# Routed attention experts: query, key and value weights held still, tokens streamed, values on the two column halves of the array

## The reference

```python
rw = _gating(hidden_states, sim_matrix, gates)          # 16 expert weights for each token
q = jnp.einsum('bte,bted->btd', rw, jnp.einsum('btc,ecd->bted', hidden_states, q_proj))
k = jnp.einsum('bte,bted->btd', rw, jnp.einsum('btc,ecd->bted', hidden_states, k_proj))
v = jnp.einsum('bte,bted->btd', rw, jnp.einsum('btc,ecd->bted', hidden_states, v_proj))
scores = jnp.einsum('bqd,bkd->bqk', q, k) * scale        # causal mask, softmax
attn = jnp.einsum('bqk,bkd->bqd', jax.nn.softmax(scores, axis=-1), v)
mixed = attn[:, :, None, :] * rw[..., None]
return jnp.einsum('bted,edc->btc', mixed, o_proj)
```

## Time and profile before

| | |
|---|---|
| runs | 1598.56, 1603.86, 1604.44 us, median 1603.86 us |
| the profiled execution's own time | 1601.31 us |
| its span, first to last instruction | 1599.5 us |
| mean granted TensorE clock | 0.935 |
| PE busy | 1390.7 us (87%) |
| PEld busy | 1019.3 us (64%) |
| DVE busy | 1144.8 us (72%) |
| ACT, POOL busy | 529.0 us, 531.6 us |
| first routed layer | about 383 to 725 us |
| second routed layer | about 1238 us to the end |

### The profile page before, as it was taken

The page is one execution under the profiler, slowest core; times in us unless marked ns, Lnnn a source line. Parts: engine busy times, 40 slices in busy tenths (PEclk is TensorE's granted clock), DMA queues, the critical chain, the costliest instruction groups (busy, mean ns, idle before and its releaser), DMA issues.

```text
span 1599.5 us, 21272 instructions
## 1 busy us (share of the span) xinstructions
PE 1390.7 (87%) x7178; PEld 1019.3 (64%) x7178; DVE 1144.8 (72%) x2582; ACT 529.0 (33%) x1015; POOL 531.6 (33%) x446
## 2 busy tenths in 40 slices
PE   2896886599999999986988988898987689999997
PEld 2793454588899999972333333343332689999996
DVE  3786674477677777532799999999998657777753
ACT  2203443210222222214556556556542022222221
POOL 1150000000000000001798999998996000000000
PEclk9998999699999999987899999999988799999999
DMA  4560000455333333300333332332331333333330
GB/s 146 208 211 0 1 1 1 145 192 194 107 107 107 107 107 107 107 1 22 101 94 87 99 99 89 99 105 86 96 105 40 107 107 113 113 113 114 114 114 14
DMA packets 93162, 155.11 MB, mean 97 GB/s; under 512 B 11703, under 2 KB 21374, under 8 KB 92926
## 3 DMA queue, kind: packets, MB, share of 16 engines
q1 hardware_dynamic: 93054, 153.76, 30.0%
HBM read 150.31 MB, written 3.41 MB: 96 GB/s over the span
## 4 chain that ended last, share of the span: by engine, by line
PE 63%; DVE 15%; issue 10%; POOL 6%; ACT 3%; DMA 2%; SPq 0%; DVEq 0%; POOLq 0%; ACTq 0%
PE bank L1103 21%; PE bank L1106 7%; PE bank L1218 6%; PE bank L960 4%; POOL both L603 3%; PE bank L991 3%; PE bank L1063 2%; DVE hs L1574 2%; PE bank L1048 2%; PE bank L1115 2%; PE bank L1157 2%; PE bank L1045 2%; DVE xe L1574 2%; DVE xe L1397 2%; PE bank L1000 2%
## 5 line engine op out<-in xcount | busy, mean ns | idle before, releaser
L1103 PE MATMUL bank<-wqkv_sb,xe 128*128 128x192 f32 x2048 | 368.4, 332 | 8.2 <-DVE xe L1517 8.2
L1103 PEld LDWEIGHTS bank<-wqkv_sb,xe 128*128 128x128 f32 x2048 | 337.5, 193 | 20.0 <-DVE xe L1517 11.3
L1218 PE MATMUL bank<-both,ident 128*128 128x512 f32 x512 | 262.3, 640 | 44.6 <-DVE both L1566 44.6
L571 POOL TENSOR_TENSOR rstd<-ve,half_neg 128x4 f32<-128x4 f32 x32 | 37.9, 1184 | 728.1 <-DVE ve L1272 728.1
L861 ACT ACTIVATE bank<-dt,A 128x512 f32<-128x512 f32 x256 | 176.1, 688 | 167.5 <-DVE hs L1574 88.9
L1218 PEld LDWEIGHTS bank<-both,ident 128*128 128x128 f32 x512 | 101.8, 206 | 172.1 <-issue 104.0
L603 POOL TENSOR_TENSOR both<-du,prT 128x512 f32<-128x512 f32 x128 | 160.9, 1272 | 7.3 <-DMA prT<-bc_dram 6.8
L1574 DVE TENSOR_TENSOR_SCAN xe<-bank,both 128x512 f32<-128x512 f32 x128 | 153.7, 1209 | 11.4 <-ACT bank L861 11.4
L603 POOL TENSOR_TENSOR both<-du,prob 128x512 f32<-128x512 f32 x128 | 160.3, 1273 | 1.9 <-DVE hs L1574 1.2
L960 PE MATMUL bank<-exp_sb,xe 128*128 128x128 f32 x1024 | 130.7, 284 | 28.8 <-DVE xe L1397 28.2
L1574 DVE TENSOR_TENSOR_SCAN hs<-bank,both 128x512 f32<-128x512 f32 x128 | 153.1, 1207 | 1.2 <-ACT bank L861 1.2
(11 more groups left out here) (256 smaller groups left out, 1978.6 us busy)
## 6 DMA issues: line engine op xcount, KB each, us to landing
dt<-w_rows SPq DMA_DIRECT2D x128, 256.0 KB, 4.1
du<-w_rows SPq DMA_DIRECT2D x128, 256.0 KB, 4.7
prob<-bc_dram SPq DMA_DIRECT2D x64, 256.0 KB, 3.3
prT<-bc_dram SPq DMA_DIRECT2D x64, 256.0 KB, 3.3
dt<-g_dram SPq DMA_DIRECT2D x32, 256.0 KB, 6.1
du<-g_dram SPq DMA_DIRECT2D x32, 256.0 KB, 6.4
g<-g_dram SPq DMA_DIRECT2D x32, 256.0 KB, 6.8
u<-g_dram SPq DMA_DIRECT2D x32, 256.0 KB, 6.7
```

The lines of the kernel that those rows point to most:

```text
L571: pool.tensor_tensor(rstd[:], ve[:], half_neg[:, 0:NT], ALU.pow).then_inc(ln_rstd, 1)
L1103: m = pe.matmul(bank[4 + j // 2][:, (j % 2) * 3 * HD:(j % 2 + 1) * 3 * HD], x_e, wqkv_sb[:, e, :], start=(e == 0 and j % 2 == 0), stop=(e ...
L1218: pe.matmul(bank[4 + k % NH][:], ident[:], hc[k % HRING], start=False, stop=(SUM_RANK[k] == sums_of(k // UNITS, k % NH))).then_inc(hc_used, 1)
```

## The change

It does four things. The experts' q and k weights (128 columns together) become the stationary operand, and the whole weighted tile of 512 tokens is streamed past them into bank 4, which now holds q and k transposed. The v weights (64 columns) of four experts are used together after every fourth expert, alternately on array columns 0 to 63 and 64 to 127, into the two halves of bank 5. ScalarE copies q and k straight into `qT`, `kT`; v goes to `vT`, is turned on TensorE by a product with `ident2`, two 64 x 64 unit matrices above and beside each other (this also adds the two halves and doubles the result), and goes from bank 0 to `v2` in one copy. The ring of weighted tiles has eight slots in place of four, and in units 0 to 15 a slot is given back with its group of four.

```diff
+                for a in range(2):
+                    chain.link(pool.tensor_tensor(ident2[:, a, :], ident[:, 0:HD], ident[:, HD:P], ALU.add))
...
                 def back(b):
-                    act.wait_ge(qkT_ps, seen(n + 1))
-                    act.activation(qT[:], bank[0][0:HD, :], ACT.Copy).then_inc(qkT_sb, 1)
-                    act.activation(kT[:], bank[0][HD:P, :], ACT.Copy).then_inc(qkT_sb, 1)
-                    yield
...
                 def qkv_copies(b):
                     act.wait_ge(xe_used, seen(experts_at(r, b) + E2))
-                    for h in range(2):
-                        qkv = bank[4 + h][:, 0:2 * 3 * HD].rearrange("p (j c) -> p j c", j=2)
-                        act.activation(qk_sb[:, 2 * h:2 * h + 2, :], qkv[:, :, 0:P], ACT.Copy).then_inc(qkv_sb, 1)
-                        for d in range(2):
-                            act.activation(v2[:, 2 * h:2 * h + 2, d, :], qkv[:, :, P:3 * HD], ACT.Copy).then_inc(qkv_sb, 1)
+                    act.wait_ge(sc_ps, seen(NT * n))
+                    act.activation(qT[:], bank[4][0:HD, :], ACT.Copy).then_inc(qkT_sb, 1)
+                    act.activation(kT[:], bank[4][HD:P, :], ACT.Copy).then_inc(qkT_sb, 1)
+                    act.activation(vT[:], bank[5][:], ACT.Copy).then_inc(vT_sb, 1)
+
+                def v_copy(b):
+                    act.wait_ge(v_turn, seen(n + 1))
+                    act.wait_ge(at_ps, seen(NT * n))
+                    act.activation(v2[:].rearrange("p j a c -> p (j a c)"), bank[0][:], ACT.Copy).then_inc(v2_sb, 1)
...
+                    if u % UNIT == E2 + 4 and 0 <= u < UNIT * NB:
+                        v_copy(u // UNIT)
...
-                    pe.wait_ge(qkv_sb, seen(6 * (n + 1)))
+                    pe.wait_ge(qkT_sb, seen(2 * (n + 1)))
+                    scores(0)
+                    yield
+                    pe.wait_ge(vT_sb, seen(n + 1))
                     pe.wait_ge(pT_sb, seen(NT * n))
                     for j in range(NT):
-                        m = pe.transpose(bank[0][:, j * P:(j + 1) * P], qk_sb[:, j, :], ident[:])
-                    m.then_inc(qkT_ps, 1)
-                    yield
-                    pe.wait_ge(qkT_sb, seen(2 * (n + 1)))
-                    scores(0)
+                        m = pe.matmul(bank[0][:, j * P:(j + 1) * P], vT[:, j * P:(j + 1) * P], ident2[:].rearrange("p a c -> p (a c)"), start=True, stop=True)
+                    m.then_inc(v_turn, 1)
                     yield
...
-                    for j in range(NT):
-                        x_e = xe[i % RING][:, j * P:(j + 1) * P]
-                        if e < E2:
-                            m = pe.matmul(bank[4 + j // 2][:, (j % 2) * 3 * HD:(j % 2 + 1) * 3 * HD], x_e, wqkv_sb[:, e, :],
-                                          start=(e == 0 and j % 2 == 0), stop=(e == E2 - 1 and j % 2 == 1))
+                    if e < E2:
+                        pe.matmul(bank[4][:], wqkv_sb[:, e, 0:P], hs[i % HRING][:], start=(e == 0), stop=(e == E2 - 1))
+                        if e % 4 == 3:
+                            for d in range(4):
+                                m = pe.matmul(bank[5][HD * (d % 2):HD * (d % 2 + 1), :], wqkv_sb[:, e - 3 + d, P:3 * HD], hs[(i - 3 + d) % HRING][:],
+                                              start=(e == 3 and d < 2), stop=(e == E2 - 1 and d >= 2))
+                            m.then_inc(xe_used, 4)
...
-                        dve.wait_ge(xe_used, seen(base + i + 1 - RING))
+                        dve.wait_ge(xe_used, seen(base + i + 1 - HRING))
```

More of the change, by code:

```diff
@@ L298, in macaron @@
         rden = sb("rden", [P, NT])
-        qk_sb = sb("qk_sb", [P, NT, P])
+        vT = sb("vT", [P, L])
+        ident2 = sb("ident2", [P, 2, HD])
         v2 = sb("v2", [P, NT, 2, HD])
@@ L336, in macaron @@
         bcT3 = wT3
[L337 removed]
+        Cs = [at2[:], vT[:]]
         xn_odd = prob[0][:].rearrange("p (j c) -> p j c", j=NT)
@@ L389, in macaron @@
             sem(n) for n in ("qk_ps", "turn_used", "frac_made", "feat_made", "v_ps", "v_made", "s_ps", "p_made"))
-        qkv_sb, qkT_ps, qkT_sb, sc_ps, nmax_made, prob_made, pT_ps, pT_sb, at_ps, at_sb = (
-            sem(n) for n in ("qkv_sb", "qkT_ps", "qkT_sb", "sc_ps", "nmax_made", "prob_made", "pT_ps", "pT_sb", "at_ps", "at_sb"))
+        vT_sb, v_turn, v2_sb, qkT_sb, sc_ps, nmax_made, prob_made, pT_ps, pT_sb, at_ps, at_sb = (
+            sem(n) for n in ("vT_sb", "v_turn", "v2_sb", "qkT_sb", "sc_ps", "nmax_made", "prob_made", "pT_ps", "pT_sb", "at_ps", "at_sb"))
         nmr_made, bank7_ps, part_ps, dlt_sb, g_made, th_made, thr_made, u_made, Du_done, ez_made, ln_made, dt_made, gates_made, \
@@ L786, in qkv_copies @@
                 def qkv_copies(b):
+                    n = r * NB + b
                     act.wait_ge(xe_used, seen(experts_at(r, b) + E2))
-                    for h in range(2):
-                        qkv = bank[4 + h][:, 0:2 * 3 * HD].rearrange("p (j c) -> p j c", j=2)
-                        act.activation(qk_sb[:, 2 * h:2 * h + 2, :], qkv[:, :, 0:P], ACT.Copy).then_inc(qkv_sb, 1)
-                        for d in range(2):
-                            act.activation(v2[:, 2 * h:2 * h + 2, d, :], qkv[:, :, P:3 * HD], ACT.Copy).then_inc(qkv_sb, 1)
-                steps = by_clock(front, 1 if layer == 3 else 0, (6, 14, 17, 19), back, (18, 22, 23, 25, 26, 28, 29, 31, 32, 34))
+                    act.wait_ge(sc_ps, seen(NT * n))
[3 more added lines that the diff above has]
+                def v_copy(b):
+                    n = r * NB + b
+                    act.wait_ge(v_turn, seen(n + 1))
+                    act.wait_ge(at_ps, seen(NT * n))
+                    act.activation(v2[:].rearrange("p j a c -> p (j a c)"), bank[0][:], ACT.Copy).then_inc(v2_sb, 1)
+                steps = by_clock(front, 1 if layer == 3 else 0, (6, 14, 17, 19), back, (22, 23, 25, 26, 28, 29, 31, 32, 34))
                 for u in CLOCK:
@@ L1052, in turned @@
                         pe.wait_ge(prob_made, seen(NT * n + t + 1))
+                        if t == 0:
+                            pe.wait_ge(v2_sb, seen(n + 1))
                         pe.wait_ge(pT_sb, seen(NT * n + t))
@@ L1098, in unit @@
                     if e == 0:
-                        pe.wait_ge(qkv_sb, seen(6 * (r * NB + b)))
-                    for j in range(NT):
-                        x_e = xe[i % RING][:, j * P:(j + 1) * P]
-                        if e < E2:
-                            m = pe.matmul(bank[4 + j // 2][:, (j % 2) * 3 * HD:(j % 2 + 1) * 3 * HD], x_e, wqkv_sb[:, e, :],
-                                          start=(e == 0 and j % 2 == 0), stop=(e == E2 - 1 and j % 2 == 1))
-                        else:
-                            m = pe.matmul(bank[7][:, j * P:(j + 1) * P], x_e, wo2_sb[:, e - E2, :],
+                        pe.wait_ge(qkT_sb, seen(2 * (r * NB + b)))
+                        pe.wait_ge(vT_sb, seen(r * NB + b))
+                    if e < E2:
[5 more added lines that the diff above has]
+                            m.then_inc(xe_used, 4)
+                    else:
+                        for j in range(NT):
+                            m = pe.matmul(bank[7][:, j * P:(j + 1) * P], hs[i % HRING][:, j * P:(j + 1) * P], wo2_sb[:, e - E2, :],
                                           start=(e == E2 and j == 0), stop=(e == UNIT - 1 and j == NT - 1))
-                    m.then_inc(xe_used, 1)
+                        m.then_inc(xe_used, 1)
                 def spread(c, k):
@@ L1516, in routed @@
                             w = bank[2 + (e - E2) % 2][:]
-                        dve.tensor_tensor(xe[i % RING][:], xnT[b % 2][:] if e < E2 else at2[:], w, ALU.mult).then_inc(xe_made, 1)
+                        dve.tensor_tensor(hs[i % HRING][:], xnT[b % 2][:] if e < E2 else at2[:], w, ALU.mult).then_inc(xe_made, 1)
                     due(steps, u)
```

## The result

The changed kernel takes 1632.05 us (median of 4 runs, 1631.55 to 1633.16), the kernel before 1601.23 us (4 runs, 1598.56 to 1604.44) on the same chip. The ratio is 1.0199, with a 95% interval of 1.018 to 1.0218: 31 us or 2.0% slower, where +49 us (1651) was forecast, in a range from 1604 to 1728 and an own range of the likeliest case from 1628 to 1668.

What follows compares the result with a forecast made beforehand. The prediction took TensorE's own instruction sequence as the bound. Its terms, 34.9 (q, k and v products) + 7.2 (turning v) - 0.6 (ScalarE) + 7.5 (VectorE wait), gave +49.0 us, 1651 us, in a range from 1604 to 1728.

Steps and rivals of the forecast that it cites:

- the likeliest case: Staggered pairing of the v products' column halves, chance 0.45: +49.0 us, 1651 us, own range 1628 to 1668.
- the five steps with their loads: In a v group, eight instructions take five steps, 2.15 us, plus 0.165 us of weight loads.
- The bound and the sign: TensorE's own sequence sets the pace in the routed layers; equal columns streamed leave nothing large to win; slower 0.80.
- The v groups: Four experts' v products: 2.15 us plus 0.165 of loads; with q and k, +0.545 us a group, +34.9 us.
- they start in program order in every row: In v groups, each product's second instruction waits for its first and holds up later ones, giving five steps.
- they pair fully: Rival for v groups: hardware sorts each half's instructions, four steps, 1.72 us; 1612 us in total; chance 0.15.
- The mode's price: Going from full array to column halves and back: taken as 0, bound 0.2 us at each change, 25.6 us.
- The turning of v: On TensorE, four fp32 products replace four transposes: +0.45 us a batch in 16 batches, +7.2 us.
- The wait for VectorE: TensorE waits 0.5 us for the tile before a batch's third expert, 15 batches: +7.5 us, bounds 0 and 12.
- ScalarE and the first batches: ScalarE's copies cost nothing except behind a layer's first batch, where scores come earlier: -0.6 us for both layers.
- The ring of eight: Eight weighted-tile slots bring nothing: the wait before the third expert is VectorE's, and elsewhere there is none to remove.
- the 1692: Top of the range for staggered pairing in the v groups with the full price of mode changes.

Runs made afterwards that it cites:

- e2: Changed kernel with all four v products of a group on one column half (old values read in the other): 1743.96 us, ratio 1.090 to the kernel before.
- e4: Changed kernel with a group's v products on halves 0, 0, 1, 1 instead of alternating, ring slots reordered: 1633.56 us, ratio 1.021 to the kernel before.
- e3: Changed kernel with k and v together as a full-width stationary in the v products (computed v wrong): 1723.75 us, ratio 1.0774 to the kernel before.
- e1: Changed kernel with v products of two experts after every second expert, not four after every fourth: 1646.33 us, ratio 1.0291 to the kernel before.
- e7: Changed kernel with v turned by four transposes instead of four fp32 products (halves not added, attention wrong): 1626.24 us, ratio 1.0174 to the kernel before.
- e6: Changed kernel with VectorE's small routing steps ahead of the scores' maximum, ring slots renamed: 1626.28 us, ratio 1.0176 to the kernel before.
- e5: Kernel before with only the ring of eight weighted tiles added: 1597.55 us against 1596.35, ratio 1.000.
- e9: Kernel before with qT and kT zero-filled to 128 rows, so the scores use the whole array: 1565.22 us, ratio 0.9779.
- e10: Kernel before with scores on zero-filled 128 rows and VectorE's small routing steps ahead of the scores' maximum: 1566.26 us, ratio 0.9788.

## Why the prediction was right, step by step

**In short.** The direction and the bound were right, the mechanism of the v groups was not, and that 1632 us lies in the own range is partly luck: the five steps with their loads were 0.60 us a group too dear (38 us in 64 groups), the missing price of the mode 0.35 too cheap (22 us), and 3.7 us came off in the scan, whose work is the same as before.

**The bound and the sign: right.** TensorE sets the pace of these stages before and after; a batch rose by 2.20 us and the two layers by 35.5. The reason given for the sign holds in part: the same number of columns is streamed, and the loads that go away were hidden (37.28 to 24.29 us of load time for nothing), so nothing was to be won. Without the price of the mode, which the forecast left out, the v groups would have cost nothing either (64 x (3.43 + 1.72 - 5.20) = -3 us), and the slowdown would have been the turning of v and the waits alone.

**The v groups: right in place, wrong in mechanism, and 0.25 us a group too dear.** Said: five steps and 0.165 us of loads, 2.31 us, no price for the mode; sum 64 x 0.545 = +34.9. Found: four steps (e2 against changed: 1.71 us saved in a group; e4: per half in order, not over both) and 0.35 us for the mode (e2 against e3; e1), 2.07 us; 64 x (3.43 + 2.07 - 5.20) = +19.2, and +17 with the mean price of 0.32. The step that failed is "they start in program order in every row". In no row of before were two matmuls on different columns, so those rows could not tell. The rival "they pair fully" had the true number of steps; it lacked the mode's price, which the prediction kept as a bound of 0.4 us a group.

**The mode's price: wrongly taken as 0.** It was read from the transposes with 16 columns, which pass without a gap. They are fp32 transposes, and the Trainium skill, "TensorEngine Tiling (Array Packing)", Restrictions, names just these as what column tiling excludes ("Transpose mode (FP32/FP32R input)"). That would explain the missing gap; no run here tests it. The rule of that page's Key Properties that a change of mode drains the engine holds here for columns as for rows: 0.09 us of emptying at each change, and an unhidden fp32 load behind it, 0.05 for 64 columns, 0.10 for 128. The scores in the earlier trace rows were the row that answered, and the prediction had read it: 0.1 of emptying and 0.1 of load.

**The turning of v: right.** +0.45 us a batch said, 0.45 in e7.

**The wait for VectorE: right in place and size, in fewer batches.** 0.5 us before the third expert said; 0.55 measured (e6), in the ten batches of steady state and not in 15: +5.5 for +7.5.

**ScalarE and the first batches: wrong in sign.** Said -0.6 us. From a layer's first expert product to that of its second batch it took 33.5 us for 30.6 in the first routed layer and 34.9 for 32.4 in the second, +2.9 and +2.5. Four v groups and the turning account for 1.65 each; the rest is 2.1 us for both layers. In the first layer it goes with waits: TensorE's idle time in this stretch rose from 3.1 to 4.4 us, 1.09 of it before the second batch's first tile (at 418.85). In the second layer the idle time did not rise (4.35 and 4.05 us), and what differs is the granted clock, 0.92 before and 0.89 after.

**The ring of eight: nothing**, as said (e5).

Together 19.2 + 7.2 + 5.5 + 2.1 = 34.0 of the 35.5 us in the two layers, or 32 with the mean price of a group. The difference is a net of larger ones. The ten batches of steady state hold 22.0 us, the first ones 5.4, the second ones 2.1 and 0.8. The last ones, up to the last output projection, hold +0.9 in the first layer and +4.3 in the second, where the terms give 1.65 each. The granted clock goes the same way, 0.89 to 0.92 in the first and 0.94 to 0.90 in the second, and e5 shows how much that can be: its batches take as long as before, its last one in the second layer 64.6 us at clock 0.87 for 61.1 at 0.94. So each of these ends can carry some 3 us that are the clock's and not the change's. The forecast of +49 is too high by 15.7 us for the v groups and 2 for the wait, and too low by 2.7 for the first batches; to the span's +31.6 the scan adds -3.7.

A slip in its range: the own range's top of 1668 counts from the runs' median, its foot of 1628 and the 1692 from the profiled time; from the latter the top is 1666.

**What stays open** is that -3.7. In the eleven other profiles the same stage takes 506.4 to 513.0 us. e9 and e10 differ only in VectorE's order in the routed layers and have 513.0 and 506.6, so it is not bound to this change. The end of the stage shows 1.5 us of it: the last eight L1218 took 5.19 us (1227.99 to 1233.18) at a mean granted clock of 0.69, and L1231 takes 3.64 (1242.68 to 1246.32) at 1.00.

```profile
1227.99:1233.18 5.19, 5.19 (x8) 2.08 (x8) 1.24 (x2) 0.00 (x0) 0.00 (x0) 0.69 0.00 0
1242.68:1246.32 3.64, 3.64 (x9) 1.44 (x9) 1.24 (x2) 0.00 (x0) 0.00 (x0) 1.00 0.00 0
```

What sets the rest was not tried.

## What to carry to other kernels

Where an engine has no idle time, price instructions from start to start and ask what a rewrite streams, not what it loads: fewer weight loads gained nothing, as they were hidden. fp32 matmuls on different column halves run truly side by side, but entering and leaving the halves costs 0.25 to 0.35 us, so they must save more than that. Here there was nothing to save: two paired halves stream as many columns as the kernel before did. And look for the same price where it is already paid: filling a 64-row contraction with zeros to 128 rows brought 2.2%.

## What the runs showed of the hardware

- Two fp32 matmuls of 64 stationary and 512 streamed columns on the two column halves start 6 to 7 ns apart (changed kernel; 12 to 13 ns in e4) and take 0.43 us together. An instruction for a free half passes those that wait for the busy one (e4).
- A change between 128 x 128 and 128 x 64, or 128 x 128 and 64 x 128, empties the array, 0.09 to 0.10 us, and the next fp32 weight load is not hidden, 0.05 us (64 columns) or 0.10 us (128). With a bf16 product behind a v group no load showed (L1128 at 493.09).
- A product with a contraction of 64 rows streams no faster than one with 128: filling them up made nothing slower, and a batch 2.15 us shorter (e9).
- The idle time that the profile gives before a matmul counts from a modelled end. The wait shown as 0.28 us cost 0.55, with the load that it laid bare.
